# The results of an attention pass turned in 32-wide blocks on VectorE, the division moved to GpSimd, its row transfers split around a free middle of each pass, and two stage borders overlapped

## The chip, the core and the metric

The kernel is one program on one core of a Trainium2 chip. Its metric is the device time of one execution in microseconds (us). The core has five engines that run their own instruction streams and meet at semaphores: TensorE (PE, with PEld for its weight loads), VectorE (DVE), ScalarE (ACT), GpSimd (POOL) and SyncE (SP, which here issues DMAs).

## The reference

One transformer layer on x of shape 8 x 1024 x 128. The normed x goes to an attention with 8 heads, 2 query and key numbers and 16 value numbers a head, and to a mixture of 16 experts, of which 12 are MLPs:

```python
xn = _layernorm(x, axis=-1)
x = x + attention(xn) + experts(xn)

# attention, per head
scores = einsum("bmhd,bnhd->bhmn", q, k) / sqrt(2)
scores = where(scores >= 0, scores, 0.2 * scores)
beta = softmax(scores, axis=-1)
out = gamma * einsum("bhmn,bnhd->bmhd", beta, v) + xn

# experts: two choices a token, 1024 slots an expert, later tokens dropped
dispatch = zeros(E, CAP, H).at[e_flat, slot].add(xn[tok] * keep)
h = gelu(einsum("ech,efh->ecf", dm, fc1_weight) + fc1_bias)      # 12 experts
out_mlp = einsum("ecf,ehf->ech", h, fc2_weight) + fc2_bias
out = (expert_out[e_flat, slot] * w).sum(choices) / gate_sums
```

## The kernel before

**Stages.** After a prologue (norm, projections, router) come attention over the first 3 sequences (`attention(0, BH)`), the 12 experts in turn, and attention over the other 5 (`attention(BH, B)`).

**A pass and its units.** An attention pass is one sequence, one group of 4 heads (`HG`) and one half of the queries (512). That makes 4 passes a sequence (`NPB`), 12 in the first stage and 20 in the last. A pass has 16 units (`UP`): 8 blocks of 128 keys, times 2 pairs of heads. TensorE's order for unit i is written out by hand:

- `shifted(i)` (L745) adds a per-query shift to the scores in PSUM, after VectorE has rectified them;
- `scores(i+2)` (L735) writes raw scores of a later unit; the ring of PSUM places holds 3 units, so it waits for the exponentials of unit i-1;
- in units 6 to 9 of a pass, one of four `turn` transposes (L775) for the pass before;
- `values` (L765) of unit i-3: four matmuls of 32 columns side by side, into the accumulator `acc[p % 2]` in PSUM.

VectorE rectifies each unit (L1030), ScalarE exponentiates it (L636, 128 x 1024 numbers). The accumulator has, for each of 4 heads, a block of 32 rows (16 values, the softmax denominator, 15 unused) by 512 queries. To bring queries to partitions, ScalarE copies it to `ot` in unit 4 (L628), TensorE transposes it back into the accumulator, VectorE takes the reciprocals of the denominators ahead of unit 12 (L1011) and multiplies ahead of unit 13 (L1016), and GpSimd adds the result to `y` (`add_attention`, L400).

**GpSimd** also moves the expert rows. In the first attention stage it sends 128 indirect DMAs (L430, `scatter`) to the expert buffers `disp`, 11 or 12 a pass. In the last stage it fetches 128 (L445, `fetch`) and adds them to `y` weighted (L457, L464, `combine`). `paced` spreads these DMAs over a pass by waiting for the count of exponentials, `value_rows` (L393) copies the value rows of a later pass into `vp` at a pass's start, and the expert stage has its own loop there.

**Stage borders.** At the first one TensorE ends the values, waits for ScalarE's copy, turns, transposes the first expert's rows (`turn_rows`, L806), and starts `expert` (L817, then L825). At the second one it computes the scores of the first two units after the last L825; the yo sum (L1042) of the last expert stands ahead of their rectification on VectorE.

**SyncE** loads q and k rows (12 DMAs a sequence and head group), expert weights and rows, and stores the sequences.

## Time and profile before

| | us |
|---|---|
| three timed runs | 976.85, 977.76, 977.84 (median 977.76) |
| the profiled execution, as timed | 976.61 |
| its span in the trace | 974.8 |
| TensorE busy | 883.5 (91%) |
| VectorE busy | 744.3 (76%) |
| ScalarE busy | 716.5 (74%) |
| GpSimd busy | 581.7 (60%) |

The busy times are of the whole span. A busy TensorE is one with matmuls in flight, and not one at its peak. The first attention stage runs from about 139 to 382 us, the experts to 562 us, the second attention stage to the end. The granted clock of TensorE is 0.974 of full speed over the span.

### The profile page before, as it was taken

What the parts mean: (1) busy time and instruction counts of PE and PEld (TensorE: products, weight loads), DVE (VectorE), ACT (ScalarE), POOL (GpSimd) and SP (SyncE); (2) the same over time, 40 slices, a digit from 0 to 9 for tenths busy, and PEclk for the clock granted to TensorE, in tenths of its full rate; (3) what the DMA queues carried; (4) which work ended last, traced back from release to release, by engine and by line L of the source; (5) the groups of instructions that cost most, each with busy time, mean ns of one, the idle gap of its engine ahead of it and who ended that gap; (6) DMA issues with size and microseconds to landing.
All of it is one profiled execution on the core that took longest, in us unless ns stands there. A gap on an engine that the chain in (4) does not pass through costs nothing.

```text
span 974.8 us, 19803 instructions
## 1 busy us (share of the span) xinstructions
PE 883.5 (91%) x7619; PEld 365.8 (38%) x7620; DVE 744.3 (76%) x851; ACT 716.5 (74%) x859; POOL 581.7 (60%) x574
## 2 busy tenths in 40 slices
PE   0688249999999999999999989999999999999997
PEld 0444102333333333867767723333333333333332
DVE  6698889999999995001011089999999999999996
ACT  0689878888888887454454468888888888888886
POOL 3355137776676662999999015647566574665770
PEclk9999659999999999999999989999999999999999
DMA  8723100101100011242342210010011002002100
GB/s 228 269 65 72 31 27 30 44 30 36 39 25 28 18 52 58 68 135 92 110 135 78 80 43 26 22 49 20 26 32 39 23 21 64 24 13 62 31 7 22
DMA packets 48163, 55.34 MB, mean 57 GB/s; under 512 B 10714, under 2 KB 35122, under 8 KB 48080
## 3 DMA queue, kind: packets, MB, share of 16 engines
q1 hardware_dynamic: 38464, 44.10, 14.8%
q0 software_dynamic: 8192, 9.37, 3.3%
q8 instruction: 54, 0.88, 0.4%
q10 hardware_dynamic: 1424, 0.76, 0.3%
q14 instruction: 29, 0.24, 0.1%
HBM read 31.58 MB, written 30.02 MB: 63 GB/s over the span
## 4 chain that ended last, share of the span: by engine, by line
PE 77%; ACT 9%; DVE 6%; issue 4%; DMA 1%; SPq 1%; POOLq 0%; ACTq 0%; DVEq 0%
PE ps L765 26%; PE ps L745 15%; PE ps L735 13%; PE ps L825 8%; PE ps L817 8%; ACT pr L636 4%; PE ps L775 3%; ACT ot L628 2%; DVE xn L897 1%; SPq L248 1%; PE ps L695 1%; PE ps L806 1%; ACT y L614 1%; DMA y<-in_x 1%; ACT va L592 1%
## 5 line engine op out<-in xcount | busy, mean ns | idle before, releaser
L1030 DVE TENSOR_SCALAR ps<-ps 128x1024 f32<-128x1024 f32 x512 | 610.7, 1229 | 20.9 <-PE ps L735 6.6
L636 ACT ACTIVATE pr<-ps 128x1024 f32<-128x1024 f32 x512 | 523.3, 1024 | 111.5 <-PE ps L745 101.0
L765 PE MATMUL ps<-pr,vp 128*32 128x256 f32 x4096 | 327.7, 392 | 0.3
L745 PE MATMUL ps<-q,kz 64*128 64x512 bf16 x1024 | 201.7, 391 | 9.2 <-DVE ps L1030 9.1
L735 PE MATMUL ps<-q,kz 62*128 62x512 bf16 x1024 | 199.9, 387 | 7.7 <-DMA q<-parts_dram 1.7
L445 POOL DMA_INDIRECT xs<-eout,idxs x128 | 129.0, 1008 | 108.7 <-ACT pr L636 78.5
L430 POOL DMA_INDIRECT disp<-xn,idx x128 | 125.6, 981 | 47.1 <-issue 35.8
L1042 DVE TENSOR_TENSOR pr<-ps,parts 128x1024 f32<-128x1024 f32 x12 | 14.7, 1225 | 166.1 <-PE ps L825 166.1
L745 PEld LDWEIGHTS ps<-q,kz 64*128 64x128 bf16 x1024 | 49.2, 93 | 222.0 <-DVE ps L1030 117.2
L765 PEld LDWEIGHTS ps<-pr,vp 128*32 128x32 f32 x4096 | 81.2, 108 | 108.1 <-issue 91.3
L663 ACT ACTIVATE pr<-ps,b1s 128x512 f32<-128x512 f32 x96 | 66.0, 687 | 48.8 <-PE ps L817 48.8
L825 PEld LDWEIGHTS ps<-w,pr 128*128 128x128 f32 x768 | 88.5, 192 | 5.7 <-issue 5.7
L825 PE MATMUL ps<-w,pr 128*128 128x128 f32 x768 | 89.5, 275 | 0.0
L817 PE MATMUL ps<-pr,w 128*128 128x512 f32 x192 | 84.5, 593 | 1.0 <-ACT pr L656 1.0
L735 PEld LDWEIGHTS ps<-q,kz 62*128 62x128 bf16 x1024 | 49.5, 93 | 93.7 <-ACT pr L636 70.4
L393 POOL COPY vp<-va 128x544 f32<-128x544 f32 x16 | 10.6, 665 | 103.4 <-PE ps L765 43.1
L542 POOL TENSOR_TENSOR y<-y,xn x24 | 56.4, 2351 | 4.9 <-POOL xn L539 4.9
L464 POOL TENSOR_TENSOR y<-y,xs 128x256 f32<-128x256 f32 x64 | 46.5, 727 | 11.7 <-POOL y L464 6.0
L817 PEld LDWEIGHTS ps<-pr,w 128*128 128x128 f32 x192 | 35.6, 191 | 41.3 <-issue 41.3
L400 POOL TENSOR_TENSOR y<-y,att 128x256 f32<-128x256 f32 x32 | 23.5, 735 | 42.2 <-DVE att L1016 40.9
L369 POOL TENSOR_TENSOR ot<-pr,parts 112x512 f32<-112x512 f32 x16 | 18.5, 1154 | 46.8 <-ACT parts L588 46.8
L656 ACT ACTIVATE pr<-ps,nw 128x512 f32<-128x512 f32 x24 | 15.2, 684 | 38.0 <-PE ps L806 38.0
(120 smaller groups left out, 618.6 us busy)
## 6 DMA issues: line engine op xcount, KB each, us to landing
disp<-pr SPq DMA_DIRECT2D x12, 512.0 KB, 4.9
eout<-pr SPq DMA_DIRECT2D x12, 512.0 KB, 2.9
y<-in_x SPq DMA_DIRECT2D x8, 512.0 KB, 8.2
out<-y SPq DMA_DIRECT2D x8, 512.0 KB
w<-in_w1t SPq DMA_DIRECT2D x12, 256.0 KB, 3.1
w<-in_w2t SPq DMA_DIRECT2D x12, 256.0 KB, 3.3
xs<-disp SPq DMA_DIRECT2D x6, 512.0 KB, 4.8
pr<-disp SPq DMA_DIRECT2D x6, 512.0 KB, 4.8
```

The lines of the kernel that those rows point to most:

```text
L430: pool.indirect_dma_start(out=disp, out_offset=bass.IndirectOffsetOnAxis(ap=idx[:, k, s * TB + t:s * TB + t + 1], axis=0), in_=xn[:, s * T ...
L445: pool.indirect_dma_start(out=g1[:, g % 2, t, c, :], out_offset=None, in_=eout, in_offset=bass.IndirectOffsetOnAxis(ap=idxs[:, c, GB * i + ...
L464: pool.tensor_tensor(yt, yt, rows[:, :, c, :], ALU.add).then_inc(S["comb" if c else "weighted"], 1)
L542: pool.tensor_tensor(yb, yb, xb, ALU.add).then_inc(S["pool_step"], 1)
L636: act.activation(pr[:, c % BUFS, 2 * pair:2 * pair + 2, :], ring[i % RING], ACT.Exp, scale=SLOPE).then_inc(S["exps"], 1)
L663: act.activation(hs[:, f, half * HALF:(half + 1) * HALF], ps[:, 2 + n % 4, :], ACT.Gelu, bias=b1s[:, u, f:f + 1]).then_inc(S["gel"], 1)
L735: last = pe.matmul(ring[i % RING][:, k, :], kz[r:r + ONES, hg, pair, kc * P:(kc + 1) * P], q2[r:r + ONES, hg, qh * HALF:(qh + 1) * HALF], ...
L745: last = pe.matmul(ring[i % RING][:, k, :], kz[r:r + TILE, hg, pair, kc * P:(kc + 1) * P], q2[r:r + TILE, hg, qh * HALF:(qh + 1) * HALF], ...
L765: last = pe.matmul(acc[p % 2][32 * g:32 * g + 32, cols], vp[:, hg, kc, g, :], pr[:, c % BUFS, g % PAIRS * 2 + g // PAIRS, cols], start=(kc ...
L817: pe.matmul(ps[:, 2 + n % 4, :], w1[:, 2 * u * FFN + f * P:2 * u * FFN + (f + 1) * P], dt_[:, half * HALF:(half + 1) * HALF], start=True, ...
L825: mm = pe.matmul(o, hs[:, f, j * P:(j + 1) * P], w1[:, (2 * u + 1) * FFN + f * P:(2 * u + 1) * FFN + (f + 1) * P], start=(f == 0), stop=(f ...
L1030: dve.tensor_scalar(s, s, 0.0, 1.0 / SLOPE - 1.0, ALU.max, ALU.mult).then_inc(S["relu"], 1)
```

## The change

- The constants `EVAC`, `TURN = 6`, `DENOM`, `FINISH` go. In 30 of 32 passes the accumulator is turned by one VectorE instruction in blocks of 32 x 32 (`dve.transpose`, PSUM to `ot`), ahead of unit 5 of the next pass; the reciprocals are taken from `ot` ahead of unit 6. A block turn leaves queries on partitions only within a block of 32, so GpSimd multiplies (`quotient`) into `att`, and SyncE puts each 32-partition piece in its place with 16 DMAs of 8 KB (`spread`, SBUF to SBUF, into `moved`). GpSimd adds a pass's result one pass later.
- The last pass of each stage (`LAST`) keeps the way of before, over ScalarE's copy and TensorE's turn.
- GpSimd's DMAs of a pass are paced in two halves, units 1 to 6 and 9 to 15. `results()` between them holds the copy of value rows, the addition for pass p-2 and the quotient of pass p-1.
- TensorE transposes the first expert's rows ahead of the last three `values`, and turns the last pass between the first expert's matmuls. ScalarE loads its function tables by a small dummy activation.
- TensorE computes the scores of units 0 and 1 of the last stage inside the last expert; VectorE rectifies them ahead of that expert's sum. ScalarE waits for the last expert's store only at unit 6.
- The last sequence is stored in two halves.

```diff
+EARLY = 6
+LATE = 9
-EVAC = 4
-TURN = 6
-DENOM = 12
-FINISH = 13
+TURN = 5
+BLOCK = 32
+NR = P // BLOCK
@@ sync
+            def spread(p):
+                sp.wait_ge(S["att_rdy"], quotients(p))
+                wait_done(sp, "y_att", p - 1)
+                for g in range(HG):
+                    for r in range(NR):
+                        sp.dma_start(moved[BLOCK * r:BLOCK * r + BLOCK, p % 2, g, :, :],
+                                     att[BLOCK * g:BLOCK * g + BLOCK, p % 2, r, :, :]).then_inc(S[f"spread{p % 2}"], 16)
...
+            for p in range(BH * NPB):
+                operands_in(p)
+                if 0 < p < BH * NPB - 1:
+                    spread(p - 1)
@@ gpsimd
+            def quotient(p):
+                pool.wait_ge(S["rg_rdy"], p + 1)
...
+                pool.tensor_tensor(att[:, p % 2, :, :, :].rearrange("p r t d -> p t r d"), rows,
+                                   inv_rows.broadcast_to([P, GT, NR, DV]), ALU.mult).then_inc(S["att_rdy"], 1)
...
-                pool.wait_ge(S["exps"], UP * p + 1 + j * (UP - 3) // count)
+                early = j < (count + 1) // 2
+                unit = 1 + j * EARLY // ((count + 1) // 2) if early else (
+                    LATE + (j - (count + 1) // 2) * (UP - 1 - LATE) // max(count // 2, 1))
+                pool.wait_ge(S["exps"], UP * p + unit)
...
+                    def results():
+                        if p % NPB == 0:
+                            value_rows(b, 1)
+                        if p % NPB == NQ and b + 1 < B:
+                            value_rows(b + 1, 0)
+                        if p > first + 1:
+                            settle(p - 2)
+                        if p > first:
+                            quotient(p - 1)
@@ scalar
                 for i in range(first, end):
-                    if i % UP == EVAC and i > first + UP:
-                        evacuate(i // UP - 1)
...
                     if i == BH * NUB:
+                        act.wait_ge(S["fc2"], E_MLP)
+                    if i == BH * NUB + (BUFS - 1) * PAIRS:
                         act.wait_ge(S["yo_out"], ONE + 16 * E_MLP)
...
+            act.wait_ge(S["pv"], BH * NPB * TB - 1)
             take_turned(0)
+            evacuate(BH * NPB - 1)
+            ready(ACT.Gelu)
@@ tensor
-                    if 0 <= i % UP - TURN < GT and i > first + UP:
-                        turn(i // UP - 1, i % UP - TURN)
...
+                if b1 == BH:
+                    pe.wait_ge(S["exps"], end - RING + 1)
+                    turn_rows(0, 0)
                 for j in range(end - 3, end):
                     values(j // PAIRS, j % PAIRS)
...
+                    if half == 1 and last:
+                        ahead(BH)
@@ vector
+            def turn(p):
+                dve.wait_ge(S["pv"], TB * (p + 1))
+                if p > 1:
+                    dve.wait_ge(S["att_rdy"], quotients(p - 2))
+                dve.transpose(ot[:, p % 2, :], acc[p % 2]).then_inc(S["turned"], 1)
...
+                    if i % UP == TURN and i > first + UP:
+                        turn(i // UP - 1)
+                    if i % UP == TURN + 1 and i > first + UP:
+                        denominators(i // UP - 1)
+                    rectify(i)
```

How instructions stand. On VectorE, one pass of before and the start of the next (`ps` is the ring and the accumulator in PSUM):

```order
L1011 RECIPROCAL rg<-ps 128x16
L1030 TENSOR_SCALAR ps<-ps 128x1024
L1016 TENSOR_TENSOR att<-ps,rg 128x256
L1030 TENSOR_SCALAR ps<-ps 128x1024 x15
L1011 RECIPROCAL rg<-ps 128x16
```

and of the changed kernel:

```order
L1124 TENSOR_SCALAR ps<-ps 128x1024 x21
L1100 STREAM_TRANSPOSE ot<-ps 128x512
L1124 TENSOR_SCALAR ps<-ps 128x1024
L1106 RECIPROCAL rg<-ot 128x16
L1124 TENSOR_SCALAR ps<-ps 128x1024 x15
```

The product has left the engine, the block turn has come, and both inserts stand seven units earlier. On TensorE, the first stage border of before, from the last unit's shift to the first expert's rows:

```order
L745 MATMUL ps<-q,kz 128x512 x2
L765 MATMUL ps<-pr,vp 32x256 x16
L775 MATMUL ps<-cst,ot 128x128 x4
L806 MATMUL ps<-cst,xs 128x128 x8
```

and of the changed kernel (L828 is `shifted`, L848 `values`, L890 `turn_rows`, L901 the experts' first matmuls, L859 the turn):

```order
L828 MATMUL ps<-q,kz 128x512 x2
L848 MATMUL ps<-pr,vp 32x256 x4
L890 MATMUL ps<-cst,xs 128x128 x8
L848 MATMUL ps<-pr,vp 32x256 x12
L901 MATMUL ps<-pr,w 128x512 x2
L859 MATMUL ps<-cst,ot 128x128 x4
L901 MATMUL ps<-pr,w 128x512 x6
```

The expert's rows moved ahead of the last values and the turn behind the first two matmuls of the expert. On TensorE, the second border of before:

```order
L825 MATMUL ps<-w,pr 128x128 x32
L735 MATMUL ps<-q,kz 128x512 x4
L745 MATMUL ps<-q,kz 128x512 x2
```

and of the changed kernel:

```order
L912 MATMUL ps<-w,pr 128x128 x16
L818 MATMUL ps<-q,kz 128x512 x4
L912 MATMUL ps<-w,pr 128x128 x16
L828 MATMUL ps<-q,kz 128x512 x2
```

The four score matmuls of the first two units moved into the last expert.

## Rows read from the trace of the kernel before

**Rows 1.** Chain that ended last: start us, us, engine, tile, line.

```profile
591.90 0.94 ACT pr L636
...
952.51 0.94 ACT pr L636
```

**Rows 2.** Timeline of two plain units: start us, us, engine line op.

```profile
666.60 0.39 PE L745 MATMUL ps<-q,kz 64*128 64x512 bf16 x2
667.03 2.13 ACT L636 ACTIVATE pr<-ps 128x1024 f32<-128x1024 f32 x2 [0.27 <-PE ps L745]
...
668.11 0.39 PE L735 MATMUL ps<-q,kz 62*128 62x512 bf16 x2
668.43 0.64 PE L765 MATMUL ps<-pr,vp 128*32 128x256 f32 x8
669.00 0.39 PE L745 MATMUL ps<-q,kz 64*128 64x512 bf16 x2
```

**Rows 3.** Timeline, ACT's copy and one of four units with a turn.

```profile
651.47 0.58 ACT L628 COPY ot<-ps 128x512 f32<-128x512 f32 x1
...
655.29 0.39 PE L745 MATMUL ps<-q,kz 64*128 64x512 bf16 x2
...
655.83 0.33 PE L775 MATMUL ps<-cst,ot 128*128 128x128 f32 x1
...
656.66 0.39 PE L745 MATMUL ps<-q,kz 64*128 64x512 bf16 x2
```

**Rows 4.** Timeline of VectorE's rectifications, and the shift that waits for one.

```profile
621.45 4.62 DVE L1030 TENSOR_SCALAR ps<-ps 128x1024 f32<-128x1024 f32 x4
...
146.72 19.33 DVE L1030 TENSOR_SCALAR ps<-ps 128x1024 f32<-128x1024 f32 x16 [0.25 <-PE ps L735]
...
666.14 3.63 DVE L1030 TENSOR_SCALAR ps<-ps 128x1024 f32<-128x1024 f32 x3
...
670.11 0.39 PE L745 MATMUL ps<-q,kz 64*128 64x512 bf16 x2
```

**Rows 5.** Groups by line and shape: out<-in, count, busy us, mean ns, idle before.

```profile
L1030 DVE TENSOR_SCALAR ps<-ps 128x1024 f32<-128x1024 f32 x512 | 610.7, 1229 | 20.9 <-PE ps L735 6.6
...
L914 DVE TENSOR_REDUCE kmax<-ps 128x1 f32<-128x512 f32 x16 | 10.9, 681 | 2.2 <-PE ps L716 2.1
L1011 DVE RECIPROCAL rg<-ps 128x16 f32<-128x16 f32 x32 | 7.9, 248 | 8.2 <-PE ps L775 8.2
...
L430 POOL DMA_INDIRECT disp<-xn,idx x128 | 125.6, 981 | 47.1 <-issue 35.8
L400 POOL TENSOR_TENSOR y<-y,att 128x256 f32<-128x256 f32 x32 | 23.5, 735 | 42.2 <-DVE att L1016 40.9
```

**Rows 6.** Timeline of the first stage border.

```profile
378.49 2.28 PE L765 MATMUL ps<-pr,vp 128*32 128x256 f32 x32
...
381.98 1.04 PE L806 MATMUL ps<-cst,xs 128*128 128x128 f32 x8
...
382.61 1.27 ACT L656 ACTIVATE pr<-ps,nw 128x512 f32<-128x512 f32 x2 [1.19 <-PE ps L806]
...
384.01 7.13 PE L817 MATMUL ps<-pr,w 128*128 128x512 f32 x16 [1.00 <-ACT pr L656]
```

**Rows 7.** Timeline of the second stage border.

```profile
562.25 0.60 PE L735 MATMUL ps<-q,kz 62*128 62x512 bf16 x4
...
564.87 0.39 PE L745 MATMUL ps<-q,kz 64*128 64x512 bf16 x2 [2.02 <-DVE ps L1030]
...
566.63 1.94 ACT L636 ACTIVATE pr<-ps 128x1024 f32<-128x1024 f32 x2
...
576.00 1.02 ACT L636 ACTIVATE pr<-ps 128x1024 f32<-128x1024 f32 x1 [0.27 <-PE ps L745]
```

**Rows 8.** Busy time (instructions) in two stretches, granted clock, DMA share, GB/s.

```profile
562.60:582.00 19.40, 15.31 (x128) 3.80 (x124) 17.25 (x15) 13.54 (x14) 4.87 (x6) 0.82 0.15 52
...
970.50:975.00 4.50, 0.00 (x0) 0.00 (x0) 0.00 (x0) 0.00 (x0) 0.63 (x1) 0.66 0.39 117
```

More of the change, by code:

```diff
@@ L239, in unit_of, with quotients, spreads @@
             return p, p // NQ % NHG, p % NQ, n // PAIRS, n % PAIRS
+        LAST = (BH * NPB - 1, B * NPB - 1)
+        def quotients(p):
+            return sum(k not in LAST for k in range(p + 1))
+        def spreads(p):
+            return sum(k not in LAST and k % 2 == p % 2 for k in range(p + 1))
         def pass_at(b, hg, qh):
@@ L770, in values, with ahead @@
                     last.then_inc(S["pv"], 1)
[L772 to L777 removed]
+            def turn(p):
+                pe.wait_ge(S["acc_evac"], 1 + LAST.index(p))
+                for t in range(GT):
+                    last = pe.transpose(acc[p % 2][:, t * P:(t + 1) * P], ot[:, p % 2, t * P:(t + 1) * P], ident)
+                last.then_inc(S["o_rdy"], 1)
+            def ahead(b):
+                for i in range(b * NUB, b * NUB + AHEAD):
+                    scores(i)
             def attention(b0, b1):
                 first, end = b0 * NUB, b1 * NUB
[L781 to L782 removed]
                 for i in range(first, end):
@@ L807, in turn_rows, with expert @@
                     last.then_inc(S["etr"], 1)
-            def expert(e, u, last):
+            def expert(e, u, first=False, last=False):
                 pe.wait_ge(S["edt"], 2 * (e + 1))
@@ L830, in expert @@
                 mm.then_inc(S["fc2"], 1)
-            turn_rows(0, 0)
-            with pe.Fori(0, E_MLP // 2 - 1) as k:
+            ahead(0)
+            attention(0, BH)
+            for u in range(2):
+                expert(u, u, first=u == 0)
+            with pe.Fori(1, E_MLP // 2 - 1) as k:
                 for u in range(2):
-                    expert(2 * k + u, u, False)
+                    expert(2 * k + u, u)
             for u in range(2):
-                expert(E_MLP - 2 + u, u, u == 1)
-            pe.wait_ge(S["gel"], ONE + 8 * E_MLP)
+                expert(E_MLP - 2 + u, u, last=u == 1)
             attention(BH, B)
+            turn(B * NPB - 1)
         @block.vector
@@ L1020, in attention @@
-            def attention(b0, b1):
-                first, end = b0 * NUB, b1 * NUB
-                for i in range(first, end):
-                    done = i // UP - 1 if i > first + UP else None
-                    if done is not None and i % UP == DENOM:
-                        denominators(done)
-                    if done is not None and i % UP == FINISH:
-                        finish(done)
-                    dve.wait_ge(S["s1"], i + 1)
-                    s = ring[i % RING]
-                    dve.tensor_scalar(s, s, 0.0, 1.0 / SLOPE - 1.0, ALU.max, ALU.mult).then_inc(S["relu"], 1)
-                denominators(end // UP - 1)
+                dve.wait_ge(S["y_att"], p - 1)
@@ new lines, in finish, with rectify, attention @@
+                dve.tensor_tensor(moved[:, p % 2, :, :, :], rows[:, :, :, 0:DV],
+                                  inv_rows.unsqueeze(3).broadcast_to([P, HG, GT, DV]), ALU.mult
+                                  ).then_inc(S["turned"], 1)
+            def rectify(i):
+                dve.wait_ge(S["s1"], i + 1)
+                s = ring[i % RING]
+                dve.tensor_scalar(s, s, 0.0, 1.0 / SLOPE - 1.0, ALU.max, ALU.mult).then_inc(S["relu"], 1)
+            def attention(b0, b1, done=0):
+                first, end = b0 * NUB, b1 * NUB
+                for i in range(first + done, end):
+                    if i % UP == TURN and i > first + UP:
[3 more added lines that the diff above has]
+                    rectify(i)
@@ L1050 @@
+            expert_rows(E_MLP - 2, 0)
+            for i in range(BH * NUB, BH * NUB + AHEAD):
+                rectify(i)
+            expert_rows(E_MLP - 1, 1)
+            attention(BH, B, AHEAD)
 _INS = ("x", "consts", "w_qk", "b_qk", "w_vr", "b_v", "r_b", "n_w", "n_w_row", "w1t", "b1", "w2t", "b2", "cvec",
```

162 lines of the change are left out of this document (91 added, 71 removed).

## The prediction

> **What bounds the kernel now.** I read the chain of waits first. It goes through the two attention stages in a fixed rhythm: the same exponential stands in it once a pass, at 591.90 and 18 passes later at 952.51 [rows 1]. A pass takes 360.61 / 18 = 20.03 us, and 32 passes make two thirds of the time. So a pass is the thing to take apart, and then the two borders of the expert stage.
>
> The timeline of a plain stretch shows what sets a unit's time. A shift starts at 666.60, ScalarE's pair of exponentials at 667.03; the first of the two ends 1.02 later, at 668.05; the scores that wait for it start at 668.11, values at 668.43, and the next but one shift at 669.00 [rows 2]. That is a closed loop: 0.43 (shift to exponential) + 1.02 + 0.06 (signal) + 0.32 (scores) + 0.57 (values) = 2.40 us for two units, 1.20 a unit. VectorE is not in it. Is it fast enough to stay out? Four rectifications in a row take 4.62, each 1.23 long [rows 4, 5], so they start (4.62 - 1.23) / 3 = 1.13 apart when nothing holds them. VectorE has 0.07 a unit to spare. And a pass with no insert on any engine, the first, has 16 of them in 19.33, (19.33 - 1.23) / 15 = 1.21 apart [rows 4]: the loop's pace, not VectorE's.
>
> What makes 20.03 of 16 x 1.20 = 19.20? In a unit with a turn, TensorE's shifts are 656.66 - 655.29 = 1.37 apart [rows 3], because TensorE is then full. Four turns cost 4 x 0.17 = 0.68. The remaining 0.15 I put down to ScalarE's copy of 0.58, which stands in the loop [rows 3].
>
> **The change in a pass.** ScalarE's copy and TensorE's four turns go from 30 of the 32 passes (the first of each stage has none before it either). TensorE and ScalarE then have 19.20 a pass. VectorE loses the product and the old reciprocals and gets the block turn T and new reciprocals R, now close together. Total work there is 16 x 1.13 + T + R, and fits. But the inserts come at once, and the loop can wait for them.
>
> No row shows a block turn. The nearest of the same size is a VectorE instruction that reads 512 columns of PSUM, 0.68 us [rows 5]; neighbours overlap by 1.23 - 1.13 = 0.10, so T = 0.59 net. Its bounds: if it went like 128 x 1024 it would be 1.13 net (above); below, it can't be under a reciprocal of 16 columns, 0.25 - 0.10 = 0.15. I take 0.59, since the row of that shape is nearest. For R I take 0.20, from the reciprocal's 0.25 [rows 5] with less overlap, since it reads SBUF now and not PSUM.
>
> The Trainium skill has a price for the block turn, which no row here can show: "VectorE: DVE Perf Modes", section "The three transpose paths", gives 311 ns for 128 x 128 in bf16. My estimate from it for 512 columns, with 1.23 - 0.68 = 0.55 per 512 columns more, is about 0.72 instead of 0.68; the sum below would then be 30 x 0.04 = 1.2 us higher.
>
> Now how late it makes the loop. In the plain rhythm rectifications start 1.13 or 1.14 and 1.26 apart in turn (three span 3.63, less 1.23 is 2.40), the later one held by its scores. That one ends at 666.14 + 3.63 = 669.77 and its shift starts at 670.11, which leaves 0.34, less 0.06 for the signal, 0.28 to spare [rows 4]; the others have some 0.15 more. Counted from the start of unit 4's, the plain rhythm has units 5, 6 and 7 at 1.26, 2.40 and 3.66. With the inserts they come at 1.13 + 0.59 = 1.72, then + 1.13 + 0.20 = 3.05, then 4.18. They are late by 0.46, 0.65 and 0.52; less what is spare (0.28, 0.43, 0.28), the shifts are late by 0.18, 0.22 and 0.24. Later units catch up at 0.07 each. These are not added up, as the delay of one moves the next: the pass is 19.20 + 0.24 = 19.44. Gain 20.03 - 19.44 = 0.59 a pass, 30 x 0.59 = **17.7 us**. With T = 1.13 it is 19.44 + 0.54 = 19.98 and the gain 1.5; with T = 0.15 nothing is late, 19.20, gain 24.9.
>
> Does the turn have to wait? The last values of a pass are issued in unit 2 of the next (unit i-3), and unit 5's insert comes behind unit 4's rectification, 2 units later: no. The buffer `ot` is freed by the quotient of two passes before, in the middle of the pass before. The rest of the way (quotient, 16 DMAs, addition) has more than a pass before anything asks for it. Behind SyncE's wait for a quotient stand only loads needed two passes later, and stores.
>
> **GpSimd.** It gets a quotient a pass, priced like the addition of the same size, 0.74 [rows 5], and loses its waits at the pass's start. A scatter pass: 128 / 11 = 11.6 DMAs, each 0.98 + 35.8 / 128 = 0.28 of issue gap [rows 5] = 1.26, so 14.7; addition and quotient with 0.2 of gap each 1.9; scaling of rows and the value copy, some 2.2 averaged. 18.8 of 19.4. It just fits; as it is paced by units 1 and 9 it may run some us late after a pass with scaling and catch up. Nobody waits soon: the nearest is the load of the first expert, which has nearly all of pass 11; I take 14 of its 19.4 us.
>
> **First border.** Before, values run 378.49 to 380.77, the expert's rows are transposed at 381.98 (1.04), ScalarE takes them (1.27) and the expert starts at 384.01 [rows 6]. After: one call of values (2.28 / 4 = 0.57) to 379.06, the transposes to 380.10, and the values of the next unit to 380.67. ScalarE waits for the second last `pv`, so it starts about 0.07 later and ends at 382.0; the expert starts at 382.05. Between its matmuls come the four turns, 0.66. Gain 384.01 - 382.05 - 0.66 = **1.3 us**. ScalarE's copy (0.6) and table load end about 384.0, before TensorE needs a result of Gelu.
>
> **Second border.** The last expert ends 562.3 [rows 7]; with 0.60 of scores inside it, 562.9. The shift is then free to start, and the first exponential comes 0.43 later, 563.35 instead of 566.63. Exponential 7 was at 576.00, 9.37 after the first instead of 7 x 1.20 = 8.40: the granted clock in that stretch is 0.82 on average [rows 8], that is partly at the lower level (1.2 GHz), and it fell after TensorE had stood for 2.02 us. After the change TensorE doesn't stand, so I take 8.40, plus 0.2 because unit 2's rectification is queued behind the sum of the last expert (1.23). 563.35 + 8.60 = 571.95, gain **4.05 us**; 3.1 if the clock falls all the same.
>
> **The end** keeps its steps. Only the last store has 256 KB instead of 512: the DMA share of 0.39 over 4.50 us is 1.76 of transfers [rows 8], half goes, **0.9 us**.
>
> **Sum.** 17.7 + 1.3 + 4.05 + 0.9 = 23.95. Against the profiled execution's own time of 976.61: 952.7. That execution lies 1.15 under the median of the runs, so a median of after may lie somewhat above; I say **953.2**.
>
> **Rivals.**
> - *The inserts count in full* (0.04). If VectorE set the pace of plain units (its rectification is 1.23 long, over 1.20), T + R = 0.79 would come on top of 19.20: 19.99, gain 1.2 in all, and 953.2 + 16.5 = 969.7. Against it: the 1.13 of four in a row.
> - *The block turn is twice as dear* (0.07), T = 1.13: 953.2 + 30 x 0.54 = 969.4. It would show in one row and so differs from the first.
> - *The loop takes nearly all of it* (0.09): T near its lower bound, or a rhythm that after a delay has more to spare. 19.20 a pass: 953.2 - 7.2 = 946.0.
> - *GpSimd falls behind, slower than before* (0.04). The place is the scatter stage. If a DMA costs more beside the 16 spread DMAs of a pass, lateness grows over 11 passes until the first expert's rows load late. It decides from (19.44 x 11 + 14) / 11 = 20.7 us of GpSimd work a pass; to eat all 24 us it takes 22.9 a pass, 4.1 more than my 18.8, so 1.61 a DMA instead of 1.26. At 1.7 a pass has 23.9 of work, 11 x (23.9 - 20.7) = 35: 988. Against it: the 0.98 of a DMA is GpSimd's own work, and SyncE issues the spread.
> - *The change does not do what it says* (0.05): some wait of the new way (the spread, the quotient) holds VectorE's turn once a pass, by about what was gained, 977.
>
> **How the numbers follow.** The forecast has 0.71, its own range 949 to 959 (T from 0.45 to 0.78, the clock, 1 us of run offset). The range for 8 in 10, 945 to 967, takes in the better case; the two cases at 969 to 970, the slower one and the last are left out, 0.20. What a measurement here can tell from no change is 0.2%, about 2 us. Faster: 0.71 + 0.04 + 0.07 + 0.09, and a little of the last, 0.92. Same 0.03, slower 0.05.
>
> **What would show it.** Right: the chain's step from pass to pass 19.4; a block turn of about 0.68; plain units still 1.20 and one late stretch behind unit 5; TensorE busy through 562 to 566 with clock 1.0; an expert stage that starts 2 us sooner. Wrong: a step of 20.0 with a short block turn (first rival), a block turn over 1.1 (second), GpSimd's DMAs late by more than a pass, or VectorE idle ahead of L1100 because of GpSimd.

## The result, and the profile after

The changed kernel takes 953.04 us (median of 4 runs, 952.74 to 954.49) where the kernel before takes 977.80 beside it (4 runs, 976.85 to 978.00). The ratio is 0.9752, with a 95% interval of 0.9735 to 0.9768: faster by 2.5%. A second measurement, e10 below, gave 953.54 against 976.91. The profiled execution took 952.74, with a span of 950.8.

The page of the changed kernel, parts 1 and 4:

```profile
PE 863.6 (91%) x7500; PEld 349.4 (37%) x7500; DVE 740.7 (78%) x851; ACT 700.7 (74%) x827; POOL 598.6 (63%) x604
...
PE 59%; DVE 31%; issue 5%; ACT 3%; DMA 1%; SPq 1%; POOLq 0%; DVEq 0%; ACTq 0%
```

TensorE lost 20 us of busy time, the turns, and VectorE 3.6; but the chain that ends last now spends 31% of the span on VectorE, where it was 6% before.

**A pass.** The chain of waits of the changed kernel (start us, us, engine, tile, line), the block turn of two passes:

```profile
831.81 0.71 DVE ot L1100
...
928.87 0.71 DVE ot L1100
```

From 831.81 to 928.87 are five passes: 97.06 / 5 = 19.41 us. By the starts of every 16th exponential the steps alternate between 19.38 and 19.47, mean 19.42, where they were 20.03 before [rows 1]. From 618 us on the block turn stands in the chain in every pass, so VectorE sets the end at that place.

The groups of the changed kernel by line and shape (as in [rows 5]):

```profile
L1124 DVE TENSOR_SCALAR ps<-ps 128x1024 f32<-128x1024 f32 x512 | 600.4, 1225 | 14.2 <-PE ps L818 11.3
...
L452 POOL TENSOR_TENSOR y<-y,moved 128x256 f32<-128x256 f32 x32 | 23.3, 730 | 46.4 <-DMA moved<-att 26.8 <-issue 14.8 <-DVE moved L1116 3.7
L1100 DVE STREAM_TRANSPOSE ot<-ps 128x512 f32<-128x512 f32 x30 | 21.2, 706 | 0.0
```

The block turn takes 706 ns, where the row that the forecast used had 681. The estimate that was worked out from the 311 ns of the Trainium skill, "VectorE: DVE Perf Modes", section "The three transpose paths", was about 0.72 us, and the trace agrees with it. VectorE never stood ahead of the block turn (0.0), so no wait of the new way reached VectorE there.

The timeline of one pass's inserts in the changed kernel (start us, us, engine line op):

```profile
637.60 0.71 DVE L1100 STREAM_TRANSPOSE ot<-ps 128x512 f32<-128x512 f32 x1
638.09 0.39 PE L828 MATMUL ps<-q,kz 64*128 64x512 bf16 x2
638.23 1.20 DVE L1124 TENSOR_SCALAR ps<-ps 128x1024 f32<-128x1024 f32 x1
639.34 0.23 DVE L1106 RECIPROCAL rg<-ot 128x16 f32<-128x16 f32 x1
...
639.49 5.72 DVE L1124 TENSOR_SCALAR ps<-ps 128x1024 f32<-128x1024 f32 x5
640.75 0.39 PE L828 MATMUL ps<-q,kz 64*128 64x512 bf16 x2
641.89 0.39 PE L828 MATMUL ps<-q,kz 64*128 64x512 bf16 x2
...
644.29 0.39 PE L828 MATMUL ps<-q,kz 64*128 64x512 bf16 x2
```

From start to start the turn takes 638.23 - 637.60 = 0.63 and the reciprocals 639.49 - 639.34 = 0.15. The shifts at 638.09 and 640.75 lie 2.66 apart instead of 2.40, so the loop came 0.26 late at this one place; from 641.89 to 644.29 it is back at 2.40. The reciprocals overlap the next instruction by 0.08; the forecast had put their overlap well under the 0.10 of the rectifications because they read SBUF now, and this row doesn't bear that out.

**The borders.** Timeline of the first border of the changed kernel:

```profile
371.97 1.09 PE L890 MATMUL ps<-cst,xs 128*128 128x128 f32 x8
373.00 1.50 PE L848 MATMUL ps<-pr,vp 128*32 128x256 f32 x24
...
375.02 1.98 PE L901 MATMUL ps<-pr,w 128*128 128x512 f32 x4 [0.52 <-ACT pr L730]
...
376.84 0.60 PE L859 MATMUL ps<-cst,ot 128*128 128x128 f32 x4
```

The last exponential of the stage starts at 371.54 and the expert's first matmul at 375.02, 3.48 later, where it was 384.01 - 378.64 = 5.37. The last values now run while ScalarE takes the expert's rows. Of the 1.89 gained, the four turns behind (0.60) take some back: 1.3. By the last Gelu of the expert stage, which starts 555.21 - 378.64 = 176.57 after that exponential before and 546.55 - 371.54 = 175.01 in the changed kernel, 1.56 are left. The second border of the changed kernel:

```profile
554.32 0.39 PE L828 MATMUL ps<-q,kz 64*128 64x512 bf16 x2
...
554.80 1.94 ACT L711 ACTIVATE pr<-ps 128x1024 f32<-128x1024 f32 x2 [6.05 <-PE ps L912]
...
558.36 0.60 PE L818 MATMUL ps<-q,kz 62*128 62x512 bf16 x2
...
564.64 1.02 ACT L711 ACTIVATE pr<-ps 128x1024 f32<-128x1024 f32 x1 [0.22 <-PE ps L828]
```

The first exponential comes 0.48 after the shift, with nothing between. But exponential 7 is at 564.64, 9.84 after the first, and was 9.37 after it before [rows 7]. From 558.36 a pair of matmuls is 0.60 long instead of 0.39. Busy time in this stretch (us, PE, PEld, DVE, ACT, POOL, granted clock, DMA share, GB/s):

```profile
558.30:561.80 3.50, 3.50 (x24) 0.64 (x22) 2.76 (x3) 2.05 (x3) 1.80 (x3) 0.52 0.26 79
```

In 3.5 us the granted clock was 0.52: the lower level, 1.2 GHz. What TensorE did just before, from 554.8 to 558.3, was to stand for 0.73, 0.57 and 0.52 us between short pairs, while VectorE took the expert's sum and then caught up. So the clock fell although the 2.02 us of idle time [rows 7] was gone. It did so in this execution, and not in the one of e10 (below). From the last addition's end, 948.10, to the end of the span are 2.72 us; before, they were 974.8 - 971.13 = 3.67.

**Where the 24 us came from**, by the starts of the same exponentials in both traces (number 0 at 139.16 in both):

| stretch | before | after | gained |
|---|---|---|---|
| first stage, exponential 0 to 191 | 239.48 | 232.38 | 7.10 |
| ... first border, experts, to 192 | 187.99 | 183.26 | 4.73 |
| seven units behind it, to 199 | 9.37 | 9.84 | -0.47 |
| the rest of the stage, to 511 | 390.01 | 378.34 | 11.67 |
| the end | 8.75 | 7.84 | 0.91 |

The sum is 23.9. Of the first row 0.35 lies in the pass without inserts (20.51 before, 20.17 after). In e10 the changed kernel's took 20.91, so this 0.35 is no work of the change. The other 6.75 / 11 and the 11.67 / 19 are both 0.614 a pass. The second row can be split at the last Gelu: 1.56 lie ahead of it, and behind it are 566.63 - 555.21 = 11.42 before and 554.80 - 546.55 = 8.25 after, 3.17 less.

### The profile page after: what moved, and what is told of

It reads as the page before. It is cut to its first block, busy times and chain, and to the rows that moved or that the text cites. A ratio compares the mean times of both kernels' runs of the same rounds, so it can differ in the third digit from the quotient of the medians.

```text
span 950.8 us, 20052 instructions
## 1 busy us (share of the span) xinstructions
PE 863.6 (91%) x7500; PEld 349.4 (37%) x7500; DVE 740.7 (78%) x851; ACT 700.7 (74%) x827; POOL 598.6 (63%) x604
## 3 DMA queue, kind: packets, MB, share of 16 engines
q0 software_dynamic: 8192, 9.37, 3.5%
## 4 chain that ended last, share of the span: by engine, by line
PE 59%; DVE 31%; issue 5%; ACT 3%; DMA 1%; SPq 1%; POOLq 0%; DVEq 0%; ACTq 0%
DVE ps L1124 22%; PE ps L848 17%; PE ps L828 11%; PE ps L818 10%; PE ps L912 9%; PE ps L901 9%; DVE ot L1100 2%; DVE xn L987 1%; PE ps L890 1%; PE ps L778 1%; DMA y<-in_x 1%; ACT y L689 1%; ACT va L667 1%; DVE bst L950 1%; ACT pr L658 1%
## 5 line engine op out<-in xcount | busy, mean ns | idle before, releaser
L1124 DVE TENSOR_SCALAR ps<-ps 128x1024 f32<-128x1024 f32 x512 | 600.4, 1225 | 14.2 <-PE ps L818 11.3
L848 PE MATMUL ps<-pr,vp 128*32 128x256 f32 x4096 | 327.7, 392 | 0.1
L828 PE MATMUL ps<-q,kz 64*128 64x512 bf16 x1024 | 201.0, 389 | 13.1 <-DVE ps L1124 7.2
L828 PEld LDWEIGHTS ps<-q,kz 64*128 64x128 bf16 x1024 | 49.1, 93 | 229.4 <-DVE ps L1124 193.7
L848 PEld LDWEIGHTS ps<-pr,vp 128*32 128x32 f32 x4096 | 81.3, 108 | 119.5 <-issue 117.8
L901 PE MATMUL ps<-pr,w 128*128 128x512 f32 x192 | 84.7, 593 | 0.5 <-ACT pr L730 0.5
L452 POOL TENSOR_TENSOR y<-y,moved 128x256 f32<-128x256 f32 x32 | 23.3, 730 | 46.4 <-DMA moved<-att 26.8
L901 PEld LDWEIGHTS ps<-pr,w 128*128 128x128 f32 x192 | 35.6, 191 | 40.6 <-issue 39.4
L403 POOL TENSOR_TENSOR ot<-pr,parts 112x512 f32<-112x512 f32 x16 | 18.5, 1155 | 46.8 <-ACT parts L663 46.8
L518 POOL TENSOR_TENSOR xs<-xs,co 128x256 f32<-128x256 f32 x64 | 37.9, 617 | 0.6
```

What stands on the lines that cost most here:

```text
L828: last = pe.matmul(ring[i % RING][:, k, :], kz[r:r + TILE, hg, pair, kc * P:(kc + 1) * P], q2[r:r + TILE, hg, qh * HALF:(qh + 1) * HALF], ...
L848: last = pe.matmul(acc[p % 2][32 * g:32 * g + 32, cols], vp[:, hg, kc, g, :], pr[:, c % BUFS, g % PAIRS * 2 + g // PAIRS, cols], start=(kc ...
L901: pe.matmul(ps[:, 2 + n % 4, :], w1[:, 2 * u * FFN + f * P:2 * u * FFN + (f + 1) * P], dt_[:, half * HALF:(half + 1) * HALF], start=True, ...
L1124: dve.tensor_scalar(s, s, 0.0, 1.0 / SLOPE - 1.0, ALU.max, ALU.mult).then_inc(S["relu"], 1)
```

## The experiments

In all runs but the repeat of the changed kernel (e10), the kernel before itself took 1078 to 1089 us (medians) on the same chip. The kernel before has no trace from there, but in the traces of all the variants that ran there, e3 and e4 among them, passes that carry GpSimd's indirect DMAs are stretched. So I give two readings: the ratio to the kernel before on that chip, and the shortest passes, which repeat within 0.04 us and show the loop alone. A "least pass" is the shortest time between the first exponentials of two passes. Passes of the two kernels alternate by 0.09 (19.38 and 19.47 in the changed one, 19.99 and 20.08 before), so a least pass is best set against the shorter of the two; the least passes of e5, e6 and e7, which keep the whole block turn, are 19.37 and 19.38. The times that were expected (946, 972 and so on) hold for a chip on which the kernel before takes 978, and such a chip came only with e10; what the others test is the pass, the borders and the end. The edits are against the changed kernel unless it says otherwise.

**e1, a small block turn.**

```diff
+            pool.memset(ot[:], 1.0)
...
-                dve.transpose(ot[:, p % 2, :], acc[p % 2]).then_inc(S["turned"], 1)
+                dve.transpose(ot[:, p % 2, 0:BLOCK], acc[p % 2][:, 0:BLOCK]).then_inc(S["turned"], 1)
...
-                dve.reciprocal(rg[:, p % 2, :], rows[:, :, DV]).then_inc(S["rg_rdy"], 1)
+                dve.tensor_scalar(rg[:, p % 2, :], rows[:, :, DV], 1.0, None, ALU.mult).then_inc(S["rg_rdy"], 1)
```

> The changed kernel with the block turn cut from 512 columns to 32 (the rest of the accumulator is left unturned, so the attention sums are left out) and the reciprocal replaced by a product of the same size. Own theory (a unit's 1.20 us is set by the loop of TensorE and ScalarE, and the block turn costs only what makes a shift late): the pass falls from 19.42 to the floor of 19.20 and no further, 30 x 0.22 = 6.6 us, so about 946. Rival (VectorE's inserts count in full): 0.5 us a pass less on VectorE is 0.5 us a pass less, 30 x 0.5 = 15, about 938, a pass of 18.9.

Measured: 1082.29 us, ratio 0.9899 (0.9842 to 0.9956). Two passes were undisturbed, 771.64 to 790.85 and this one (columns as above):

```profile
838.31:857.52 19.21, 19.13 (x194) 5.61 (x192) 19.02 (x19) 16.39 (x16) 6.68 (x8) 1.00 0.15 40
```

The turn of 32 columns takes 208 ns, and the pass falls to 19.21. The whole lateness of a pass, 0.21 of the mean and 0.17 of the least pass, belongs to the size of the block turn, and below it stands the loop at 16 x 1.20.

**e2, a second block turn** into a spare tile, ahead of the first.

```diff
+        spare = sb("spare", [P, 2, HALF])
...
+                dve.transpose(spare[:, p % 2, :], acc[p % 2])
                 dve.transpose(ot[:, p % 2, :], acc[p % 2]).then_inc(S["turned"], 1)
```

> The changed kernel with a second block turn of the same accumulator into a spare tile, ahead of the first. Own theory: the slack of the rhythm is used up by the first, so the second, 0.63 us from start to start, is late in full: pass 20.05, 30 x 0.63 = 19 us more, about 972. Rival (the cost of the block turn is not lateness but something else, as contention): less than half of it, under 962.

Measured: 1087.06 us, ratio 0.9966 (0.9931 to 1.0001). The least pass:

```profile
769.97:789.94 19.97, 19.14 (x194) 5.50 (x192) 19.85 (x20) 16.39 (x16) 6.84 (x9) 1.00 0.08 20
```

A second turn, 0.60 from start to start, makes the pass 19.97 - 19.42 = 0.55 longer (0.59 against the least pass): nearly in full. The first one costs 0.21 of its 0.63, since the loop had room for the rest. So the price isn't proportional: it starts where the room ends. VectorE is busy for 19.85 of the 19.97.

**e3, before without TensorE's turns** (against the kernel before).

```diff
-                    if 0 <= i % UP - TURN < GT and i > first + UP:
-                        turn(i // UP - 1, i % UP - TURN)
...
-                for t in range(GT):
-                    turn(end // UP - 1, t)
...
```

> The kernel before with TensorE's turn transposes left out (VectorE works on the unturned accumulator, its reciprocal replaced by a product of the same size; the attention sums are left out). VectorE's inserts and ScalarE's copy stay where they were. Own theory: units 6 to 9 fall from 1.37 to 1.20, 0.68 a pass, 30 passes 20.4 and 2 x 0.66 at the stage ends: about 956, a pass of 19.35. Rival (VectorE sets the pace of a unit): its work is the same, so a pass of 20.0 and about 976.

**e4, and without ScalarE's copy too** (against e3).

```diff
-                    if i % UP == EVAC and i > first + UP:
-                        evacuate(i // UP - 1)
...
-                evacuate(end // UP - 1)
...
```

> As the last one, with ScalarE's copy of the accumulator left out too. Own theory: a further 0.15 a pass, 4.5 us, and 2 x 0.7 at the stage ends, the floor of 19.20 a pass: about 950. Rival (the 0.15 belongs to VectorE's own inserts ahead of units 12 and 13): a pass stays at 19.35 and the time at 955.

Measured: e3 1075.09 us, ratio 0.9871 (0.9825 to 0.9917); e4 1073.46, ratio 0.9854 (0.9810 to 0.9897). Least passes of e3, then of e4:

```profile
828.87:848.38 19.51, 19.32 (x194) 5.67 (x194) 19.15 (x19) 16.75 (x18) 7.41 (x9) 1.00 0.05 12
```

```profile
828.02:847.23 19.21, 19.13 (x194) 5.61 (x192) 18.78 (x18) 16.39 (x16) 7.41 (x9) 1.00 0.06 12
```

The turns were worth 20.03 - 19.51 = 0.52 (0.48 of the shorter passes), not 0.68, and the copy 19.51 - 19.21 = 0.30, not 0.15. The sum, 0.82, is within 0.01 of the prediction's. ScalarE's timeline in e3 shows why the copy isn't the small one:

```profile
769.61 1.02 ACT L636 ACTIVATE pr<-ps 128x1024 f32<-128x1024 f32 x1 [0.27 <-PE ps L745]
770.53 0.58 ACT L628 COPY ot<-ps 128x512 f32<-128x512 f32 x1
771.00 2.04 ACT L636 ACTIVATE pr<-ps 128x1024 f32<-128x1024 f32 x2
```

The second of a plain pair starts 2.13 - 1.02 = 1.11 after the first [rows 2], so the one behind the copy was due at 770.72 and starts at 771.00, 0.28 late. The pass ends 0.30 later than in e4: what the copy delays, the loop does not catch up.

**e5, no early scores** (the second border of before, in the changed kernel).

```diff
-                    if half == 1 and last:
-                        ahead(BH)
...
+            ahead(BH)
             attention(BH, B)
...
-            for i in range(BH * NUB, BH * NUB + AHEAD):
-                rectify(i)
             expert_rows(E_MLP - 1, 1)
-            attention(BH, B, AHEAD)
+            attention(BH, B)
```

> The changed kernel with the scores and rectifications of the last stage's first two units put back behind the last expert. Own theory: the first exponential again comes 4.3 us after the last expert matmul instead of 0.4, less 0.6 of scores inside the expert: 3.3 us slower, about 956.4, and the clock falls in either case. Rival (what was gained there is given back by the clock or by the wait for the last store): under 1 us, about 954.

**e6, no early expert turn** (the first border of before).

```diff
-            act.wait_ge(S["pv"], BH * NPB * TB - 1)
-            take_turned(0)
             evacuate(BH * NPB - 1)
+            take_turned(0)
...
-                if b1 == BH:
-                    pe.wait_ge(S["exps"], end - RING + 1)
-                    turn_rows(0, 0)
...
+            turn(BH * NPB - 1)
+            turn_rows(0, 0)
```

> The changed kernel with the first expert's rows transposed behind the last pass's turn, in the order of before. Own theory: 1.3 to 1.5 us slower, about 954.5. Rival (the loads of the second expert, or ScalarE's table load, decide when the expert goes on): within 0.5 us of 953.

Measured: e5 1088.36 us, ratio 1.0014 (0.9978 to 1.0050); e6 1086.19, ratio 0.9968 (0.9936 to 1.0001). Those ratios can't tell 1 or 3 us. The expert stage, which is not stretched, can. From the last exponential of the first stage to the first of the second, e5 and then e6:

```profile
449.59:635.42 185.83, 182.66 (x1100) 134.12 (x1094) 17.06 (x16) 85.38 (x128) 140.71 (x66) 1.00 0.31 99
```

```profile
451.48:635.96 184.48, 182.71 (x1102) 134.31 (x1097) 16.90 (x16) 85.58 (x128) 140.70 (x66) 1.00 0.31 98
```

The changed kernel has 183.26 there, so 2.57 and 1.22 seem to be lost. But these are single executions, and the eight others that keep both borders of the changed kernel (e1, e2 and e7 to e12) have 183.17 to 183.42 and, in e7 and e8, 184.12 and 184.00. So the parts have to be looked at. For e6, ScalarE's instructions come 1.22 later than in the changed kernel from the middle of the stage to its end. For e5, the timeline of TensorE has this ahead of the last expert:

```profile
613.80 1.09 PE L890 MATMUL ps<-cst,pr 128*128 128x128 f32 x8 [0.72 <-DMA pr<-disp]
```

The last expert's rows came late by DMA, which held the stage by 0.9. The same wait makes e7 and e8 long by 1.0 and 0.6, and they keep the early scores. So it is not what the early scores are worth. The stretch behind it is clean: from the last Gelu to the first exponential, in the kernel before, the changed kernel and e5:

```profile
555.21 0.69 ACT L663 ACTIVATE pr<-ps,b1s 128x512 f32<-128x512 f32 x1 [0.17 <-PE ps L817]
```

```profile
546.55 0.69 ACT L737 ACTIVATE pr<-ps,b1s 128x512 f32<-128x512 f32 x1 [0.17 <-PE ps L901]
```

```profile
625.37 0.69 ACT L737 ACTIVATE pr<-ps,b1s 128x512 f32<-128x512 f32 x1 [0.17 <-PE ps L901]
```

To the first exponential it is 11.42 before, 8.25 in the changed kernel (and in all nine other traces with early scores, e6's too), and 635.42 - 625.37 = 10.05 in e5. So the early scores are worth 10.05 - 8.25 = 1.80, and 11.42 - 10.05 = 1.37 of the border's 3.17 is a part that both keep. The kernel before has this on ScalarE, beside the shift of [rows 7] at 564.87:

```profile
565.33 1.28 ACT L636 ACT_TABLE_LOAD   x1 [9.44 <-PE ps L745]
```

and of e5 this:

```profile
634.93 0.39 PE L828 MATMUL ps<-q,kz 64*128 64x512 bf16 x2 [1.92 <-DVE ps L1123]
...
635.42 1.02 ACT L711 ACTIVATE pr<-ps 128x1024 f32<-128x1024 f32 x1 [7.85 <-issue]
```

From the shift to the exponential it was 566.63 - 564.87 = 1.76 before and is 635.42 - 634.93 = 0.49 in e5: 1.27 are the function table, which the changed kernel and e5 load ahead (`ready`). The forecast had this gain, since it put the exponential 0.43 behind the shift, but it didn't name where it came from. TensorE stands for 1.92 in e5, and the clock falls there as before.

**e7, GpSimd in the order of before**: evenly paced, value rows copied at a pass's start, addition and quotient behind the DMAs.

```diff
-                early = j < (count + 1) // 2
-                unit = 1 + j * EARLY // ((count + 1) // 2) if early else (
-                    LATE + (j - (count + 1) // 2) * (UP - 1 - LATE) // max(count // 2, 1))
-                pool.wait_ge(S["exps"], UP * p + unit)
+                pool.wait_ge(S["exps"], UP * p + 1 + j * (UP - 3) // count)
...
-                    def results():
-
-                        if p % NPB == 0:
-                            value_rows(b, 1)
...
-                    move(p, results)
+                    if p % NPB == 0:
+                        value_rows(b, 1)
+                    if p % NPB == NQ and b + 1 < B:
+                        value_rows(b + 1, 0)
+                    move(p, lambda: None)
+                    if p > first + 1:
+                        settle(p - 2)
+                    if p > first:
+                        quotient(p - 1)
```

> The changed kernel with GpSimd's order of before: value rows at the start of a pass, DMAs evenly spaced, the addition and the quotient behind them at the pass's end. Own theory: GpSimd is nowhere on the path, so the time stays within 1 us of 953. Rival (the free middle carries part of the gain: a late quotient makes SyncE's transfers, the buffers or the first expert's load late): 3 us or more slower, with VectorE idle ahead of the block turn or TensorE idle ahead of the first expert.

Measured: 1112.31 us, ratio 1.0210 (1.0148 to 1.0272): slower, and whether by 2% is unclear. Its sisters e5, e6 and e8, on the same chip, took 1085 to 1088, 24 to 27 us less. So the order of GpSimd's work was worth 2.2 to 2.5% there, and the expectation, within 1 us, was wrong. Its least pass, from 851.99 to 871.37, is 19.38 like the changed kernel's.

The waits of e7 (engine, line waited for: us, times, longest):

```profile
DVE ps L1118 <- remote: 69.0, 28, 4.5
...
POOL vp L427 <- PE ps L842: 46.3, 10, 10.1
```

and of e5, for the rectification:

```profile
DVE ps L1123 <- remote: 45.6, 20, 4.3
```

GpSimd's copy of value rows waits for the values of the pass before (46.3 us in ten copies) while its DMAs are queued behind it; the changed kernel's copies, and e5's, wait for no values. Then it sends most DMAs of a pass one behind the other. In the passes nobody is shown waiting for GpSimd, and a pass that isn't stretched is no longer for it.

At the end of the kernel somebody does wait. GpSimd's last instructions in e7:

```profile
1095.94 0.62 POOL L439 TENSOR_TENSOR att<-ot,rg 128x256 f32<-128x256 f32 x1
1107.91 1.40 POOL L452 TENSOR_TENSOR y<-y,moved 128x256 f32<-128x256 f32 x2 [11.35 <-issue]
```

The quotient of the last pass but one stands behind that pass's work and starts 1.28 us ahead of the last exponential (1097.22), where it starts 9.51 ahead in the changed kernel; its 16 transfers come behind it, and only then the last additions. From the last exponential to the end of the span it is 15.09 here and 15.38 in e12, against 7.84 in the changed kernel and e5. These 7.25 us do not hang on stretched passes. The rest lies in the two attention stages, against e5, e6 and e8 some 9 to 14 us in the first and 9 to 11 in the last, in more waits of VectorE that the profile can only call remote.

**e8 and its repeats e9 and e11, the block turn in two halves**, ahead of units 5 and 9, the reciprocals ahead of 10.

```diff
-                dve.transpose(ot[:, p % 2, :], acc[p % 2]).then_inc(S["turned"], 1)
+                dve.transpose(ot[:, p % 2, 0:HALF // 2], acc[p % 2][:, 0:HALF // 2])
+
+            def turn_rest(p):
+
+                dve.transpose(ot[:, p % 2, HALF // 2:HALF], acc[p % 2][:, HALF // 2:HALF]).then_inc(S["turned"], 1)
...
-                    if i % UP == TURN + 1 and i > first + UP:
+                    if i % UP == TURN + 4 and i > first + UP:
+                        turn_rest(i // UP - 1)
+                    if i % UP == TURN + 5 and i > first + UP:
                         denominators(i // UP - 1)
```

> The changed kernel with the block turn in two halves of 256 columns, ahead of units 5 and 9, and the reciprocals ahead of unit 10. Own theory: a half is about 0.36 from start to start, 0.23 late against the rhythm, under the 0.28 that is spare, and four units on the lateness is caught up: a pass at the floor of 19.20, 30 x 0.22 = 6.6 us faster, about 946.5. Rival (VectorE's inserts count in full): 0.1 us a pass more work, 3 us slower, 956. A third outcome: GpSimd's quotient, now after unit 10, makes its DMAs late, and some of the gain is lost in the first stage.

> The block turn in two halves once more, since in the first comparison the kernel before itself took 1087 us and whole passes were stretched by waits that belong to no kernel. Where passes were left alone there, the step was 19.21. Own theory: where the kernel before takes 978, this one takes 946.5 (19.20 a pass). Rival (inserts count in full): 956.

> The block turn in two halves, now that the kernel before takes 977 again. Own theory: 19.20 a pass, 30 x 0.22 = 6.6 us under the changed kernel's 953.5, about 947, ratio to the kernel before 0.969. Rival (VectorE's inserts count in full): 3 us slower than the changed kernel, 956, ratio 0.979.

Measured: 1085.28 us, ratio 0.9983 (0.9950 to 1.0017); 1075.31, ratio 0.9972 (0.9944 to 0.9999); 1078.49, ratio 0.9981 (0.9947 to 1.0015). The timeline of VectorE in a least pass of e8, and that pass:

```profile
776.48 0.44 DVE L1100 STREAM_TRANSPOSE ot<-ps 128x256 f32<-128x256 f32 x1
776.84 4.59 DVE L1128 TENSOR_SCALAR ps<-ps 128x1024 f32<-128x1024 f32 x4
781.34 0.43 DVE L1104 STREAM_TRANSPOSE ot<-ps 128x256 f32<-128x256 f32 x1
781.70 1.20 DVE L1128 TENSOR_SCALAR ps<-ps 128x1024 f32<-128x1024 f32 x1
```

```profile
772.69:791.91 19.22, 19.14 (x194) 5.58 (x192) 19.14 (x20) 16.39 (x17) 6.87 (x9) 1.00 0.11 28
```

Two halves cost 0.36 each from start to start, 0.09 more than the whole, and yet the pass is at 19.21: a delay of 0.36 goes into the room that the loop has, a delay of 0.63 doesn't. By its passes this version would gain 30 x 0.17 to 0.21 = 5 to 6 us over the changed kernel where passes aren't stretched. But the reciprocals come five units later and the quotient behind them, so its end is longer: from the last exponential 10.05, 9.45 and 9.52 us in the three runs, against 7.84. That takes back 1.6 to 2.2. The two repeats ran on chips that stretched the passes too: its time on a chip like the first stays open.

**e10, the changed kernel again**, unedited.

> The changed kernel itself, to have it beside the variants on a chip where the kernel before takes 1075 to 1090 us. If the kernel before takes 978 again, this takes 953, ratio 0.975. If it takes over 1070: own theory, the gain of 24 us was made of TensorE's turns, ScalarE's copy and the borders, which are still gone, so the stretches that are left alone step by 19.4 against 20.0, but a stretch that waits for something else gains nothing, so the ratio is nearer to 1, about 0.985 to 1.0. Rival (the waits come from the 16 transfers a pass that the change adds): the ratio is over 1.01.

Measured: 953.54 us (952.16 to 956.51), before 976.91, ratio 0.9759 (0.9733 to 0.9786), steps of 19.38 and 19.47. Passes were not stretched on this chip, so the run says nothing on the chips that do. But its profiled execution differs at the second border. From exponential 192 to 199:

```profile
558.07:566.48 8.41, 6.54 (x62) 1.71 (x58) 8.41 (x8) 7.06 (x8) 2.30 (x3) 1.00 0.33 108
```

The seven units take 8.41 instead of 9.84, at a granted clock of 1.00, although TensorE stood for the same 0.73, 0.57 and 0.52 us. In ten traces with the early scores these three gaps are the same, and the clock fell in two (the changed kernel's and e1's). In the four traces without them (before, e3, e4, e5), with a gap of 1.9 to 2.0, it fell in all four. What decides between the two outcomes of the same gaps, no run here shows.

**e12, e7 again** on a third chip.

> The changed kernel with GpSimd's order of before, now that the kernel before takes 977 again. Own theory as first stated: GpSimd is nowhere on the path, within 1 us of 953.5. Rival (the free middle carries part of the gain): 3 us or more slower, most of it in the first stage, where GpSimd's work fills a pass and the value copy at a pass's start makes it wait.

Measured: 1104.60 us, before 1078.14, ratio 1.0220 (1.0167 to 1.0272). The chip stretched passes again, so this repeats e7. It tells what the order costs on a chip that doesn't only at the end, 15.38 against 7.84.

## Why the prediction was right

The forecast was 953.2, the median 953.04. Term by term, against the profiled execution:

| step | predicted | measured | from |
|---|---|---|---|
| pass | 19.44 | 19.42 | steps of the exponentials |
| 30 passes | 17.7 | 18.4 | 30 x 0.614 |
| pass without inserts | 0 | 0.35 | 20.51 - 20.17; 20.91 in e10 |
| first border | 1.3 | 1.56 | up to the last Gelu; e6 1.22 |
| second border, first exponential | 3.28 | 3.17 | 11.42 - 8.25; 1.80 for the scores (e5), 1.27 for the table load |
| second border, the seven units behind | 0.77 | -0.47 | 9.37 - 9.84; +0.96 in e10 (8.41) |
| the end | 0.9 | 0.91 | 8.75 - 7.84 |

The terms miss by +0.7, +0.35, +0.26, -0.11, -1.24 and 0, and the misses cancel. So a sum that is right to 0.1 us is luck; that it is right to 1 or 2 us is not.

- **The closed loop of 1.20 a unit, with VectorE just outside: shown.** e1, e4 and e8 take away different things (turn size, turns and copy, the turn's length in one piece) and all have least passes of 19.21.
- **The block turn makes the loop late once, by 0.24: shown.** T was 0.63 instead of 0.59, R 0.15 instead of 0.20; the two errors nearly cancel in T + R, and the lateness was 0.21 by the mean pass and 0.26 by the shifts. e2 bounds it from above, e8 shows that it hangs on one delay being longer than the room for it. The rival "inserts count in full" needed 19.99, and "twice as dear" a turn of 1.13; neither came.
- **What a pass lost before, 0.83, was right in sum and wrong in its parts.** I had put 0.68 to the turns by multiplying one unit's excess by four and left the copy the rest. e3 and e4 give 0.52 and 0.30. The sum came out because the copy had been given whatever was left above the floor of 19.20. The parts did not matter, because the change removes both.
- **The passes' gain is 0.7 larger than predicted**, 0.02 a pass: the passes came 0.22 over 19.20, where I had 0.24.
- **The step that is wrong as stated is the clock at the second border**: "After the change TensorE doesn't stand, so I take 8.40". It doesn't stand for 2 us, but it does for three times 0.5 to 0.7, the first behind the exponentials, the others behind VectorE, which has the expert's sum (1.22) and then units 2 to 5 to catch up on. In the compared execution the clock fell to 1.2 GHz for 3.5 us all the same, and the seven units took 9.84. In e10 they had the same gaps and no fall, and took 8.41, under the 8.60 of the forecast. So the number could come true, and whether it does changes from one execution to the next, by 1.43 us. The forecast should have had a chance for each. Its bound, 3.1 if the clock falls, was for the whole border and measured 3.17 - 0.47 = 2.7.
- **GpSimd "just fits, nobody waits": right for the changed kernel, and e7 shows how little is behind it.** The pass from 159.33 (row below) has 14.99 us of GpSimd busy with 12 to 13 DMAs in it, each with 0.30 of issue gap, which makes 18.6 to 18.9 against the 18.8 of the forecast, and a DMA takes 983 ns where it took 981 before. The quotient and DMAs ran up to some microseconds late, as paced, and the `moved` tile kept GpSimd for 26.8 us in all without effect. But the order of GpSimd's work decides 7.25 us at the end of the kernel, and 2.2 to 2.5% in all on the chips that stretch passes; that the quotient of the last pass but one must be early was nowhere in the forecast. My price for the transfers beside the loop, zero, is shown only for the chips of the first measurement and of e10. I can't say what the changed kernel takes on a stretching chip, as it was not run on one; e5 and e6, which are it but for 1 to 3 us, tied there with the kernel before. So, as far as these two stand for it, **on those chips the gain is given back**, and the cause is open.

**What stays open: the stretched passes.** They go with the indirect DMAs: in e8, passes in which 4 of them start took 19.21 twice (772.69 to 791.91 is shown above), and the one with 10 between those took 26.59. The four others with 4 took 19.36 to 21.65, and the first stage's, with 9 to 15, took 20.98 to 31.35. The pass of 26.59, and the second of those of 19.21:

```profile
813.29:839.88 26.59, 20.97 (x184) 5.15 (x182) 19.42 (x19) 16.29 (x17) 17.26 (x22) 0.87 0.16 38
839.88:859.09 19.21, 19.13 (x194) 5.61 (x192) 19.17 (x20) 16.39 (x17) 6.68 (x8) 1.00 0.15 40
```

The changed kernel, where 12 DMAs start in the pass from 159.33, took 19.47, with VectorE and ScalarE busy as long:

```profile
159.33:178.80 19.47, 19.28 (x194) 5.62 (x192) 19.41 (x19) 16.37 (x16) 14.99 (x15) 1.00 0.11 33
```

The stretched pass has about the same DMA share as the one behind it and no more GB/s, so the amount of data does not explain it. How a stretch looks, from e1's timeline:

```profile
158.74 0.39 PE L830 MATMUL ps<-q,kz 64*128 64x512 bf16 x2
...
161.12 1.02 ACT L713 ACTIVATE pr<-ps 128x1024 f32<-128x1024 f32 x1 [3.33 <-remote]
161.16 1.23 DVE L1126 TENSOR_SCALAR ps<-ps 128x1024 f32<-128x1024 f32 x1 [3.12 <-remote]
...
162.20 0.61 PE L820 MATMUL ps<-q,kz 62*128 62x512 bf16 x2 [3.07 <-ACT pr L713]
```

TensorE's scores (157.84) and shift were done by 159.1, and ScalarE and VectorE both went on two microseconds later, within 0.04 of each other, while GpSimd kept sending a DMA each 1.28. TensorE then had stood for 3 us, and its next pair took 0.61, the lower clock. It looks as if a signal to two engines came late together; that is an argument from one row, and no run took the DMAs away on such a chip. The last pass of a stage, which has none, took 17.7 to 18.5 there up to its last exponential (e2 with its second turn 18.8), near the changed kernel's 17.9.

## What to carry to other kernels

When engines form a loop with a fixed pace, find for each the room that it has in one unit, and cut an insert to fit: a block turn in halves cost more of VectorE and less of the pass (19.21 against a least pass of 19.38), and a second whole one cost nearly its full 0.60. Then look at the end of the kernel, where work that is late without effect in every pass is waited for once (7.25 us in e7). Price an overlap at a border with the queue of the engine that is asked to do both things, since gaps of 0.5 to 0.7 us were followed here by a lower TensorE clock for 3.5 us in two executions of ten. And compare a kernel only with one that ran on the same chip, but look at its least stretches as well: they carried a difference of 0.2 us a pass through runs in which other passes were stretched by up to 13 us.

## What the runs showed of the hardware

- A block turn on VectorE of 128 x 512 in float32 from PSUM takes 706 ns, of 128 x 256 440 and of 128 x 32 208, with 0.08 of that beside the next instruction. Both steps are 0.27 per 256 columns, near the 1.23 - 0.68 = 0.55 per 512 columns of the instructions that read PSUM [rows 5].
- Small SBUF to SBUF DMAs kept SyncE for 0.7 us each, one behind the other. In the changed kernel, SyncE's queue:

```profile
362.25 9.82 SPq L332 DMA_DIRECT2D moved<-att  x14
```

Fourteen take 9.82, so the 16 of a pass fill 11 of its 19.4 us of SyncE. By this estimate a second such set of 16 in a pass would not fit.

- TensorE's granted clock after the same gaps of 0.73, 0.57 and 0.52 us fell to 0.5 for about 3.5 us in two traces and stayed at 1.00 in eight; after a gap of 1.9 to 2.0 us it fell in four of four.
- A function table load on ScalarE took 1.28 us, and 1.27 us less passed between shift and exponential when it was loaded ahead.
- The kernel before took 977 to 978 us in the first measurement and beside e10, and 1078 to 1089 (medians) on the four chips of the other runs, 10 to 11% more. In the traces of the kernels run there, the passes with indirect DMAs are the stretched ones, and the expert stage isn't.
